# Four superblocks of 128-row tiles in place of two of 256-row tiles, with a shared PSUM bank and rows loaded eight tiles ahead

## The chip, the cores and the metric
The kernel runs on one core of a Trainium2 chip, in one launch. The metric is the device time in microseconds. All arithmetic is in 32-bit floats. The engines are TensorE (PE; its weight loads are PEld), VectorE (DVE), ScalarE (ACT), GpSimd (POOL) and SyncE (SP, which here only issues DMAs). TensorE writes to eight PSUM banks of 128 partitions by 512 floats.

## The reference
The input x is 32 batches of 128 rows by 128 features; the context is 32 x 120 x 128.
```python
x = x + tanh(g_xattn[0]) * attention(layernorm(x), ctx, ctx, ..., mask)   # 16 heads of 8, softmax over 120 keys
z = layernorm(x)                                        # 4096 rows
scores = z @ gate_w + gate_b                            # 8 experts
vals, idx = top_k(scores, 2); p = softmax(vals)
h = relu(einsum('td,edf->etf', z, w1) + b1)             # 512 hidden features
y = einsum('etf,efd->etd', h, w2) + b2
x = x + tanh(g_ffn[0]) * sum over the two experts of p * y
```
Only the two chosen experts of a row count, so 8192 pairs of row and expert have to be computed.

## The kernel before
**Attention.** The batches go in 8 groups of four (G). The work of a group is cut into 8 slots, t = 8G + s; a slot computes the scores of two units (a unit is four heads of one batch) and carries the two units of the slot before on. Scores go to one of four banks A, VectorE takes row maxima (`row_max`), ScalarE the exponentials (`exps`), TensorE transposes them (`transposes`, line 503) into bank T or U, and VectorE and ScalarE copy them to SBUF in turns (`copy_pt`). In odd slots TensorE multiplies a finished batch by the values (`values`, line 516) and sums (`sums`, line 524) into bank O; VectorE unloads O with a reciprocal (line 923) and a multiply (line 927, `unload`). Other small products of a group, such as projections, transposes of the next group and gate scores, are "entries" of given slots (`EXTRAS`).

**Routing.** Once group G is through attention, VectorE adds the residual and statistics, GpSimd normalises (`z2`), the gate scores pick two experts, and `route` gives each row a place in a DRAM buffer ordered by expert (`zs`). GpSimd scatters the 2 x 512 rows of a group with 8 indirect DMAs (line 809). Groups are joined into superblocks; before, two of four groups each (`SB = (4, 4)`). When the last group of a superblock is ranked, VectorE computes a table (`table`, lines 1008 to 1033) that says for each tile which expert and which rows it has. The number of tiles is fixed for the worst case: 23 tiles of 256 rows per superblock.

**Expert tiles.** SyncE waits for the table, then for each tile reads the expert and row from SBUF into registers, loads the expert's packed weights (`wbuf`, 578 KB, line 409) and the tile's rows (`zin`, 128 KB, line 413), four tiles ahead, and stores results to `ys` (line 420). TensorE transposes the rows into bank Y (line 577), VectorE moves them to `zT` (line 1040), TensorE multiplies by w1 (`first_product`, line 593) in two halves of two 128-feature chunks into bank U, ScalarE evicts with bias and relu into `H` (line 722), TensorE multiplies by w2 into Y (`second_product`, line 604), VectorE adds the bias (`yo`, line 1046). A tile is cut into four sub-steps, `sub(b, k)`.

**Order.** Every engine executes the same hand-written list of slots in its own program order; semaphores join them. The sub-steps of the first superblock are put into slots 42 to 71, three per slot. Attention's last scores are in slot 63; the slots up to 71 let the last group's routing drain. After slot 71 the rest of the first superblock and all 23 tiles of the second follow alone. In the first superblock's time U belongs to the experts, and attention is left with T alone; afterwards T is a second bank for first products. When all stores of a superblock have landed, GpSimd gathers for each of its batches and choices the 128 result rows (line 818), and VectorE adds them, weighted, to x (`combine`, line 1064); SyncE writes each finished group out. All gathers come after the slots, those of the second superblock after its last tile.

## Time and profile before
| | |
|---|---|
| median of 3 runs | 677.74 us (669.64 to 679.08) |
| profiled execution, whole | 671.73 us |
| its span, first to last instruction | 669.7 us |
| mean granted TensorE clock (1 is 2.4 GHz) | 0.911 |
| TensorE busy, share of the span | 527.6 us, 79% |
| VectorE busy | 290.7 us, 43% |
| ScalarE busy | 269.9 us, 40% |
| GpSimd busy | 256.7 us, 38% |
| moved by DMA | 78.75 MB, mean 118 GB/s |

The shares are means over stages: start, slots without expert work, slots with it, expert tiles alone, and gathers. An idle stretch of an engine is listed with what ended it; "issue" means that the profile shows nothing for which the engine waited. A group's "busy" counts overlapping instructions once, so that it can be less than count times mean.

### The profile page before, as it was taken

How to read it: one execution, taken by the hardware profiler on the slowest of the kernel's cores; microseconds unless marked ns; L12 is line 12 of the kernel's file. 1: busy time of each engine (PE TensorE's matmuls, PEld its weight loads, DVE VectorE, ACT ScalarE, POOL GpSimd, SP SyncE). 2: the span in 40 equal slices, each digit the busy share in tenths (PEclk: the TensorE clock that was granted, in tenths of full speed). 3: DMA queues.
4: the chain of work that ended last, by engine and by line, in shares of the span. 5: the costliest groups of instructions: out<-in, count | busy, mean ns of one | idle time of the engine just before them, and what ended most of it. 6: DMA issues, size and time to landing. Idle time of an engine off the chain costs nothing.

```text
span 669.7 us, 12645 instructions
## 1 busy us (share of the span) xinstructions
PE 527.6 (79%) x4481; PEld 379.2 (57%) x4481; DVE 290.7 (43%) x899; ACT 269.9 (40%) x812; POOL 256.7 (38%) x281
## 2 busy tenths in 40 slices
PE   1699999999989997898989898988838768878000
PEld 1265656566555654566767676676736667667000
DVE  2236648448557566344544555353331222321122
ACT  1256555446446552454555454642302333333000
POOL 6623063284454654332217022302453333200574
PEclk9779989789989986898999999999977999989655
DMA  5999790000000003311313131324426676663122
GB/s 127 285 418 241 244 374 2 17 17 11 9 17 18 2 17 84 123 52 52 119 53 116 55 120 54 119 70 154 133 71 209 202 208 207 206 174 122 51 82 71
DMA packets 60971, 78.75 MB, mean 118 GB/s; under 512 B 8421, under 2 KB 46573, under 8 KB 60909
## 3 DMA queue, kind: packets, MB, share of 16 engines
q1 hardware_dynamic: 56813, 69.55, 34.1%
q0 software_dynamic: 4096, 8.40, 4.1%
q8 instruction: 36, 0.59, 0.4%
q14 instruction: 26, 0.21, 0.1%
HBM read 46.73 MB, written 35.93 MB: 123 GB/s over the span
## 4 chain that ended last, share of the span: by engine, by line
PE 35%; issue 34%; SPq 13%; DMA 9%; POOL 4%; ACT 3%; DVE 2%; POOLq 0%; ACTq 0%
PE Y L604 11%; DMA zin<-zs 8%; PE U L593 7%; POOL yg L818 4%; SPq L391 4%; PE A L491 4%; PE T L503 3%; PE O L524 2%; PE A L495 2%; ACT H L722 2%; SPq L389 2%; PE T L593 2%; PE Y L577 1%; PE O L516 1%; SPq L386 1%
## 5 line engine op out<-in xcount | busy, mean ns | idle before, releaser
L687 ACT ACTIVATE P<-A,nmax 128x120 f32<-128x120 f32 x512 | 135.6, 386 | 13.8 <-DVE nmax L911 13.8
L911 DVE TENSOR_REDUCE nmax<-A 128x4 f32<-128x480 f32 x128 | 78.1, 652 | 110.2 <-PE A L495 96.2
L491 PE MATMUL A<-Kb,Q 32*128 32x480 f32 x256 | 102.3, 640 | 8.9 <-ACT P L687 6.1
L722 ACT ACTIVATE H<-U,wbuf 128x256 f32<-128x256 f32 x138 | 57.9, 471 | 121.0 <-PE U L593 118.3
L604 PE MATMUL Y<-wbuf,H 128*128 128x128 f32 x736 | 97.8, 285 | 9.4 <-issue 5.3
L809 POOL DMA_INDIRECT zs<-z,posu x64 | 63.2, 987 | 101.4 <-DVE posu L985 85.8
L604 PEld LDWEIGHTS Y<-wbuf,H 128*128 128x128 f32 x736 | 93.0, 199 | 15.9 <-issue 8.4
L818 POOL DMA_INDIRECT yg<-ys,ypos x64 | 60.4, 944 | 107.2 <-DMA ys<-yo 50.7
L593 PE MATMUL U<-zT,wbuf 128*128 128x256 f32 x276 | 74.6, 394 | 12.4 <-ACT H L722 11.7
L771 POOL TENSOR_TENSOR rstd<-mv,eps 128x4 f32<-128x4 f32 x16 | 3.2, 197 | 174.5 <-DVE mv L895 174.5
L503 PE MATMUL T<-I,P 128*120 128x128 f32 x352 | 55.9, 283 | 10.4 <-DVE PT L917 6.9
L593 PEld LDWEIGHTS U<-zT,wbuf 128*128 128x128 f32 x276 | 48.0, 194 | 20.6 <-ACT H L722 14.8
L503 PEld LDWEIGHTS T<-I,P 128*120 128x120 f32 x352 | 43.4, 144 | 22.8 <-issue 19.4
L917 DVE COPY PT<-T 120x512 f32<-120x512 f32 x64 | 43.8, 684 | 28.1 <-PE T L503 27.4
L1046 DVE TENSOR_TENSOR yo<-Y,wbuf 128x256 f32<-128x256 f32 x46 | 19.4, 423 | 81.0 <-PE Y L604 80.4
L491 PEld LDWEIGHTS A<-Kb,Q 32*128 32x128 f32 x256 | 30.3, 190 | 42.7 <-ACT P L687 28.4
L788 POOL TENSOR_SCALAR Kb<-Kt,hm 128x480 f32<-128x480 f32 x32 | 46.9, 1477 | 18.6 <-ACT Kt L708 18.6
L694 ACT COPY PT<-U 120x512 f32<-120x512 f32 x40 | 23.4, 586 | 74.0 <-PE U L503 65.2
L778 POOL TENSOR_SCALAR z<-X,mv,rstd 128x128 f32<-128x128 f32 x64 | 50.2, 791 | 3.0 <-POOL rstd L773 2.7
L495 PE MATMUL A<-mb_r,I_r 128*128 128x480 f32 x128 | 48.7, 464 | 0.0
L495 PEld LDWEIGHTS A<-mb_r,I_r 128*128 128x128 f32 x128 | 20.3, 199 | 48.0 <-issue 48.0
L1040 DVE COPY zT<-Y 128x256 f32<-128x256 f32 x46 | 19.4, 422 | 55.8 <-PE Y L577 50.4
(127 smaller groups left out, 613.3 us busy)
## 6 DMA issues: line engine op xcount, KB each, us to landing
wbuf<-wpk SPq DMA_DIRECT2D x46, 578.0 KB
zs<-zero SPq DMA_DIRECT2D x2, 9216.0 KB, 31.1
zin<-zs SPq DMA_DIRECT2D x46, 128.0 KB
ys<-yo SPq DMA_DIRECT2D x46, 128.0 KB
wpk<-in_w SPq DMA_DIRECT2D x1, 2048.0 KB, 35.0
wpk<-in_w SPq DMA_DIRECT2D x8, 256.0 KB, 10.7
out<-X SPq DMA_DIRECT2D x8, 256.0 KB
ctx_sb<-in_ctx SPq DMA_DIRECT2D x1, 1440.0 KB, 16.8
```

Source lines behind the costliest of these rows:

```text
L491: mm(a[:, 0:HG * LK].rearrange("p (j k) -> p j k", j=HG), Q[r, G % 2, i * LQ:(i + 1) * LQ], Kb[r, G % 2, :, i * LK:(i + 1) * LK], start=Tr ...
L495: mm(bank("S", n)[:, 0:HG * LK].rearrange("p (j k) -> p j k", j=HG), I_r[:], mb_r[:].unsqueeze(1).broadcast_to((128, HG, LK)), start=False ...
L503: last = nc.tensor.transpose(t[0:LK, j * LQ:(j + 1) * LQ], P[:, n % 4, j, :], I[:])
L593: last = mm(u_bank(b, half)[:, (c % 2) * TS:(c % 2 + 1) * TS], wbuf[:, n % NW, c * 128:(c + 1) * 128], zT[:, n % 2, :], start=True, stop=True)
L604: last = mm(Yb[:, h * 128:(h + 1) * 128], H[:, n % 2, c, h * 128:(h + 1) * 128], wbuf[:, n % NW, FF + c * D:FF + (c + 1) * D], start=(c == ...
L687: ins = nc.scalar.activation(P[:, n % 4, j, :], a[:, j * LK:(j + 1) * LK], ACT.Exp, bias=nmax[:, n % 4, j:j + 1])
L722: nc.scalar.activation(H[:, n % 2, c, :], u[:, (c % 2) * TS:(c % 2 + 1) * TS], ACT.Relu, bias=wbuf[:, n % NW, W_B1 + c:W_B1 + c + 1]).then ...
L778: ins = nc.gpsimd.tensor_scalar(dst[:, i, :], batch_x(G, i), mv[:, i, 0:1], r[:, 1, i:i + 1], ALU.subtract, ALU.mult)
L788: ins = nc.gpsimd.tensor_scalar(Kb[:, G % 2, j, :], Kt[:], hm[:, j:j + 1], None, ALU.mult)
L809: nc.gpsimd.indirect_dma_start(out=zs[sb_of(F)], out_offset=bass.IndirectOffsetOnAxis(ap=posu[:, F, k, i:i + 1], axis=0), in_=z2[:, F % 2, ...
L818: nc.gpsimd.indirect_dma_start(out=yg[:, n % NYG, :], out_offset=None, in_=ys[b], in_offset=bass.IndirectOffsetOnAxis(ap=ypos[:, i // GB, ...
L911: v.tensor_reduce(nmax[:, n % 4, :], bank("S", n)[:, 0:HG * LK].rearrange("p (j k) -> p j k", j=HG), AX_X, ALU.max, negate=True).then_inc( ...
```

## The change
There are four superblocks of two groups, and tiles have 128 rows. That gives 23 tiles per superblock and 92 in all. `SUBS`, `RATE` and `DRAIN_RATE` plan the steps: a tile has two, `first_product` (four chunks of 128 columns, one bank) and `y_step` (the second product of the tile before and the transpose of the rows two tiles on). Four steps go into an even slot, two into an odd one, and other numbers into slots 65 to 71. The first superblock starts in slot 26, the second in 42, the third in 58; 10 steps of the third and all of the fourth come after the slots.

`y_step` writes the upper half of bank O, whose lower half holds a batch's values and sums; so bank Y is gone and T has two banks, which attention alternates to the end. In the last steps, T's banks alternate with O and U. Before a step on O, TensorE waits for the unload of the last batch; before the values of a batch it waits until VectorE has emptied the last step. Weights are loaded five tiles ahead, rows eight, in separate functions; the next superblock's may be asked for during the last tiles of one. The two `zs` buffers are used in turns and are half as long. Of the gathers, 21 go into slots from 43 on, one per slot. In the last group of a superblock, rank, place and scatter come one slot earlier.
```diff
-SB = (4, 4)
+SB = (2, 2, 2, 2)
-TS = 256
+TS = 128
-NW = 4
+NW = 5
+NZ = 8
-SUBS = [4 * (n + 1) for n in NTB]
-SUB_FIRST = NS * (SB[0] + 1) + 2
-SUB_RATE = 3
+SUBS = [2 * (n + 1) for n in NTB]
+RATE = (4, 2)
+DRAIN_RATE = {65: 2, 66: 4, 67: 4, 68: 2, 69: 2, 70: 2, 71: 0}
...
-        Tb = ps("T")
+        Tb = [ps(f"T{r}") for r in range(2)]
         Ob = ps("O")
         Ub = ps("U")
-        Yb = ps("Y")
...
+        def u_bank(n):
+            return Tb[1] if late_tile(n) else Ub
+        def y_bank(m):
+            return Tb[0] if late_step(m) else Ob
...
             def transposes(n):
                 freed(pe, "S", n)
-                copied(pe, n - 2 if n <= LAST_U + 1 else n - 1)
+                copied(pe, n - 2)
...
                 pe.wait_ge(o_free, k + 1)
+                if begun["step"] is not None:
+                    wait(pe, yo_done, YO_THROUGH[begun["step"]])
+                    wait(pe, zt_done, ZT_THROUGH[begun["step"]])
...
+            def first_product(b, i):
+                n = N0[b] + i
+                pe.wait_ge(w_in[n % NW], 16 * (n // NW + 1))
+                pe.wait_ge(zt_done, zt_of(b, i))
+                ...
+                for c in range(NC):
+                    last = mm(u_bank(n)[:, c * TS:(c + 1) * TS], wbuf[:, n % NW, c * 128:(c + 1) * 128],
                               zT[:, n % 2, :], start=True, stop=True)
...
+            def y_step(b, i):
+                m, n = STEP[b, i], N0[b]
+                y = y_bank(m)
+                ...
+                if not late_step(m):
+                    pe.wait_ge(o_free, begun["batches"] + 1)
+                    begun["step"] = m
+                if moves_y(b, i):
+                    n = N0[b] + i - 1
+                    pe.wait_ge(h_done, NC * (n + 1))
+                    for c in range(NC):
+                        last = mm(y[:, 2 * TS:3 * TS], H[:, n % 2, c, :],
+                                  wbuf[:, n % NW, FF + c * D:FF + (c + 1) * D], start=(c == 0), stop=(c == NC - 1))
+                ...
+                elif moves_z(b, i):
+                    last = tile_transpose(y, N0[b] + i + 2, 3 * TS)
+                last.then_inc(y_ready, 1)
...
+            def load_w(n):
+                ...
+                wait(sp, yo_done, n - NW + 1)
+                e = sp.value_load(tab[0:1, b, 1, i:i + 1], min_val=0, max_val=NE - 1)
+                sp.dma_start(wbuf[:, n % NW, :], wpk[bass.ds(e, 1)].squeeze(0)).then_inc(w_in[n % NW], 16)
+            def load_z(n):
+                b, i = tile_of(n)
+                if i == 0:
+                    for q in range(2):
+                        sp.wait_ge(scat[q], 16 * 2 * GB * ((LAST[b] + 1 - q) // 2))
+                if n >= NZ:
+                    sp.wait_ge(zt_done, zt_of(*tile_of(n - NZ)))
+                row = sp.value_load(tab[0:1, b, 0, i:i + 1], min_val=0, max_val=ROWS - TS)
+                sp.dma_start(zin[:, n % NZ, :], zs[b % NZS][bass.ds(row, TS)]).then_inc(z_in[n % NZ], 16)
...
             for b in range(NB):
+                for i in range(-1, NTB[b]):
+                    if i >= 0:
+                        store(b, i)
+                    known = N0[b + 1]
+                    if b + 1 < NB and SLOT_OF.get((b, 2 * i + 3), NEVER) > NS * LAST[b + 1] + NS - 1:
+                        known = N0[b + 2]
+                    if i >= 0 or b == 0:
+                        while w_next < min(N0[b] + i + 1 + NW, known):
+                            load_w(w_next)
+                            w_next += 1
+                        while z_next < min(N0[b] + i + 1 + NZ, known):
+                            load_z(z_next)
+                            z_next += 1
...
# VectorE, in slot(G, s): moved behind routing and tables
+                for key in ks[1 if odd else 3:]:
+                    sub(*key)
+                if t in PRE:
+                    y_step(PRE[t], None)
+                for n in GATHER_AT.get(t - GATHER_LAG, ()):
+                    combine(n)
```

## Rows read from the trace of the kernel before

**Rows 1.** The timeline of VectorE: start, duration, engine, line, count, [idle before <-releaser].
```profile
170.49 0.95 DVE L923 RECIPROCAL orec<-O 128x128 f32<-128x128 f32 x1
226.81 0.96 DVE L923 RECIPROCAL orec<-O 128x128 f32<-128x128 f32 x1 [0.48 <-PE O L524]
...
266.63 0.96 DVE L923 RECIPROCAL orec<-O 128x128 f32<-128x128 f32 x1 [0.70 <-PE O L524]
...
457.87 0.96 DVE L923 RECIPROCAL orec<-O 128x128 f32<-128x128 f32 x1 [3.18 <-PE O L524]
```
**Rows 2.** Windows: stretch, length, each engine's busy time, granted clock, DMA share, GB/s.
```profile
170.50:227.00 56.50, 52.68 (x515) 32.75 (x514) 34.49 (x106) 30.41 (x98) 28.44 (x32) 0.97 0.03 11
335.70:446.70 111.00, 102.32 (x971) 76.31 (x972) 52.87 (x155) 56.72 (x174) 28.96 (x30) 1.00 0.28 86
505.50:621.30 115.80, 93.47 (x596) 80.94 (x596) 27.40 (x77) 38.45 (x92) 26.39 (x28) 0.97 0.61 185
```
**Rows 3.** The timeline of TensorE, one expert tile after the slots.
```profile
565.87 0.44 PE L577 MATMUL Y<-I,zin 128*128 128x128 f32 x2 [0.29 <-DMA zin<-zs]
566.14 1.03 PE L593 MATMUL T<-zT,wbuf 128*128 128x256 f32 x4
567.00 1.95 PE L604 MATMUL Y<-wbuf,H 128*128 128x128 f32 x16
568.79 1.03 PE L593 MATMUL U<-zT,wbuf 128*128 128x256 f32 x4
```
**Rows 4.** Waits by pair, 504 to 622 us: total, times, longest.
```profile
PE Y L577 <- DMA zin<-zs: 28.1, 16, 7.2
```
**Rows 5.** The timeline at the last tile's eviction and the next two gathers.
```profile
620.84 0.42 DVE L1046 TENSOR_TENSOR yo<-Y,wbuf 128x256 f32<-128x256 f32 x1 [2.21 <-PE Y L604]
623.92 0.94 POOL L818 DMA_INDIRECT yg<-ys,ypos  x1 [46.09 <-DMA ys<-yo]
625.17 0.94 POOL L818 DMA_INDIRECT yg<-ys,ypos  x1 [0.30 <-issue]
```
**Rows 6.** Waits of TensorE, 325 to 455 us.
```profile
PE U L593 <- ACT H L722: 6.5, 7, 1.2
PE Y L604 <- ACT H L722: 2.2, 4, 0.6
```
**Rows 7.** Costliest groups: line, shapes, count | busy, mean ns | idle before, releaser.
```profile
L687 ACT ACTIVATE P<-A,nmax 128x120 f32<-128x120 f32 x512 | 135.6, 386 | 13.8 <-DVE nmax L911 13.8
...
L503 PE MATMUL T<-I,P 128*120 128x128 f32 x352 | 55.9, 283 | 10.4 <-DVE PT L917 6.9
```
**Rows 8.** Groups by shape: the unload of bank O on VectorE.
```profile
L923 DVE RECIPROCAL orec<-O 128x128 f32<-128x128 f32 x32 | 30.6, 957 | 23.0 <-PE O L524 23.0
L927 DVE TENSOR_TENSOR OT<-O,orec 128x128 f32<-128x128 f32 x32 | 9.3, 292 | 1.1
```
**Rows 9.** The timeline around the first table.
```profile
252.13 0.21 DVE L1008 TENSOR_TENSOR tcmp<-jt,A 128x64 f32<-128x64 f32 x1
257.89 1.08 PE L503 MATMUL T<-I,P 128*120 128x128 f32 x4 [3.49 <-issue]
```
**Rows 10.** The timeline between the two superblocks.
```profile
485.12 0.17 DVE L985 CAST posu<-posf 128x8 uint32<-128x8 f32 x1
504.32 0.69 PE L577 MATMUL Y<-I,zin 128*128 128x128 f32 x2 [7.17 <-DMA zin<-zs]
```
**Rows 11.** The timeline of SyncE in the lone tiles: a store and the loads behind it.
```profile
599.72 0.37 SPq L420 DMA_DIRECT2D ys<-yo  x1
601.41 0.35 SPq L409 DMA_DIRECT2D wbuf<-wpk  x1
601.94 0.37 SPq L413 DMA_DIRECT2D zin<-zs  x1
```
**Rows 12.** SyncE's weight loads at the start of the second superblock.
```profile
502.02 0.35 SPq L409 DMA_DIRECT2D wbuf<-wpk  x1
504.59 0.02 SPq L409 DMA_DIRECT2D wbuf<-wpk  x1
507.51 0.00 SPq L409 DMA_DIRECT2D wbuf<-wpk  x1
```

More of the change, by code:

```diff
@@ L40 @@
 LAST = [SB0[b] + SB[b] for b in range(NB)]
-TS = 256
-TH = TS // 128
+TS = 128
 NTB = [(2 * n * TOK + NE * (TS - 1)) // TS for n in SB]
-N0 = [sum(NTB[:b]) for b in range(NB)]
+N0 = [sum(NTB[:b]) for b in range(NB + 1)]
 NTM = max(NTB)
 CAP = max(SB) * TOK
+NJ = CAP // TS
 ROWS = NE * CAP + NE * TS
+NZS = 2
 W_B1 = FF + NC * D
@@ L60, with slot_plan @@
 ZROW = 8 * D
-SUBS = [4 * (n + 1) for n in NTB]
-SUB_FIRST = NS * (SB[0] + 1) + 2
-SUB_RATE = 3
-LAST_U = 2 * (SUB_FIRST - 2) - 1
 DRAIN = NS * NG + NS
+NIT = 48
+SUBS = [2 * (n + 1) for n in NTB]
+RATE = (4, 2)
+DRAIN_RATE = {65: 2, 66: 4, 67: 4, 68: 2, 69: 2, 70: 2, 71: 0}
+NEVER = 10 ** 6
+def slot_plan():
+    subs, pre, t = {}, {}, 0
+    for b in range(NB):
+        k, t = 0, max(t, NS * (LAST[b] + 1) + 2)
+        if t < DRAIN:
+            pre[t - 1] = b
+        while k < SUBS[b] and t < DRAIN:
+            n = DRAIN_RATE.get(t, RATE[t % 2])
+            subs[t] = [(b, j) for j in range(k, min(k + n, SUBS[b]))]
+            k, t = k + n, t + 1
+    return subs, pre
@@ new lines, with moves_z, moves_y @@
+PLAN, PRE = slot_plan()
+SLOT_OF = {key: t for t, keys in PLAN.items() for key in keys}
+PLANNED = [sum(1 for key in SLOT_OF if key[0] == b) for b in range(NB)]
+STEPS = [(b, i) for b in range(NB) for i in [None] + list(range(NTB[b] + 1))]
+STEP = {key: m for m, key in enumerate(STEPS)}
+LATE = NS * NG + 2
+def moves_z(b, i):
+    return i is None or i + 2 < NTB[b]
+def moves_y(b, i):
+    return i is not None and i >= 1
+ZT_THROUGH = [sum(1 for key in STEPS[:m + 1] if moves_z(*key)) for m in range(len(STEPS))]
@@ new lines, with step_slot, late_step @@
+YO_THROUGH = [sum(1 for key in STEPS[:m + 1] if moves_y(*key)) for m in range(len(STEPS))]
+def step_slot(b, i):
+    if i is None:
+        return {c: t for t, c in PRE.items()}.get(b, NEVER)
+    return SLOT_OF.get((b, 2 * i + 1), NEVER)
+LATE_STEP = min(m for m, key in enumerate(STEPS) if step_slot(*key) >= LATE)
+LATE_TILE = min(N0[b] + i for b in range(NB) for i in range(NTB[b]) if SLOT_OF.get((b, 2 * i), NEVER) >= LATE)
+def late_step(m):
+    return m >= LATE_STEP and (m - LATE_STEP) % 2 == 0
@@ new lines, in late_tile, with prior, tile_of, zt_of @@
+def late_tile(n):
+    return n >= LATE_TILE and (n - LATE_TILE) % 2 == 0
+def prior(n, late):
+    return max([m for m in (n - 1, n - 2) if m >= 0 and late(m) == late(n)], default=None)
+def tile_of(n):
+    b = max(b for b in range(NB) if N0[b] <= n)
+    return b, n - N0[b]
+def zt_of(b, i):
+    return ZT_THROUGH[STEP[b, None if i < 2 else i - 2]]
+NGATHER = 2 * B
+GATHER_LAG = 3
+def gather_plan():
+    plan, n = {}, 0
+    for b in range(NB - 1):
+        ends = [SLOT_OF.get((b, k), NEVER) for k in range(SUBS[b])]
+        t = max(ends) + 2
+        while n < 2 * GB * LAST[b] and t + GATHER_LAG < NS * NG + 3:
+            c = min(GATHER_RATE, 2 * GB * LAST[b] - n)
+            plan[t] = list(range(n, n + c))
+            n, t = n + c, t + 1
+    return plan, n
@@ L589, in first_product @@
+                before = prior(n, late_tile)
+                if before is not None:
+                    pe.wait_ge(h_done, NC * (before + 1))
+                if n == LATE_TILE:
                     copied(pe, NG * NP - 1)
-                else:
-                    wait(pe, h_done, NC * n - 2 + 2 * half)
-                for c in (2 * half, 2 * half + 1):
-                    last = mm(u_bank(b, half)[:, (c % 2) * TS:(c % 2 + 1) * TS], wbuf[:, n % NW, c * 128:(c + 1) * 128],
+                for c in range(NC):
+                    last = mm(u_bank(n)[:, c * TS:(c + 1) * TS], wbuf[:, n % NW, c * 128:(c + 1) * 128],
@@ L800, in scatter @@
                 if part == 0:
-                    if F in SB0:
-                        pool.wait_ge(zs_clear[sb_of(F)], 16)
+                    b = sb_of(F)
+                    if F in SB0 and b < NZS:
+                        pool.wait_ge(zs_clear[b], 16)
+                    elif F in SB0:
+                        for q in range(NZ):
+                            pool.wait_ge(z_in[q], 16 * sum(1 for n in range(N0[b - NZS + 1]) if n % NZ == q))
                     pool.wait_ge(z2_done, F + 1)
@@ L836, in slot @@
                     residual_base(G)
[L837 removed]
+                for n in GATHER_AT.get(t, ()):
+                    gather(n)
+                if s == 6:
                     if G + 2 < NG:
```

306 lines of the change are left out of this document (134 added, 172 removed).

## The prediction
> **What bounds the kernel now.** I read the reciprocals of the attention batches first, because one falls in every second slot and so times the slots. Batches 11 and 16 stand 56.3 us apart, 11.3 us per pair of slots without expert work; batches 19 and 31 stand 191.2 us apart, 15.9 us per pair with six expert steps in it [rows 1]. Next the windows by stage. TensorE is busy 102.3 of 111.0 us in the filled slots and 52.7 of 56.5 us in the empty ones; VectorE, ScalarE and GpSimd are at half or less in the filled ones. After the slots TensorE falls to 93.5 of 115.8 us [rows 2]. So the slots are paced by TensorE's in-order queue, and an expert tile hidden in them is not free. A pair pays 15.9 - 11.3 = 4.6 us for 1.5 tiles of 256 rows, about 3.1 us a tile. In the second superblock's lone stage a tile takes 115.8 / 23 = 5.0 us, although its own TensorE work is shorter: transposes 0.27, two half first products of 0.86, second product 1.79, together 3.8 us [rows 3]. The rest is the wait for rows, 28.1 us in 16 waits [rows 4]. Last, the end: from the last eviction of an expert tile (ending 621.3) to the end of the span are 48.4 us, in which 32 gathers go out 1.25 us apart [rows 5].
>
> The profiled execution took 671.7 us, 669.7 of span and 2.0 around it. The median of the runs, 677.7, is 6.0 above it, and their own spread is 9.4; I sum against 671.7.
>
> **The change, part by part.**
>
> *Same rows, other places.* Both versions process 46 x 256 = 92 x 128 rows. With four superblocks the slots take expert work from slot 26 instead of 42, still three steps' worth of rows per two half tiles, and only 5 tiles of the third superblock and 23 of the fourth (28 x 128 rows) are left for the end, against 1.5 + 23 tiles of 256 before.
>
> *TensorE columns.* A first product now streams 128 columns per weight load instead of 256. Rows at 128 columns exist: 16 in 1.79 us is 0.112 us each; the 256-column ones take 0.86 / 4 = 0.215 [rows 3]. A 128-row tile therefore costs 0.14 + 8 x 0.112 + 8 x 0.112 = 1.93 us, two of them 3.86 against 3.78: +0.12 us per pair of slots.
>
> *First-product bank.* Four chunks of 128 fit one bank, so the second half no longer waits for the eviction of the first. That wait and the second product's like it cost 6.5 + 2.2 us in the 130 us from 325 to 455 [rows 6], 8.2 pairs: -1.06 us per pair.
>
> *Transpose banks.* The alternation of two banks stays where before one was left. In the filled slots of before the single one cost nothing visible (the wait on VectorE's copy is 6.9 us, in all such rows of the whole span [rows 7], and none of the idle time from 325 to 455), since expert work stands between. I take 0, bounds 0 and -7 us.
>
> *The shared bank.* This is the new wait. In an odd slot the expert step after the sums needs the unload: 0.47 us until VectorE starts [rows 1], 0.96 reciprocal, 0.29 multiply [rows 8], some 0.13 between and after: 1.85 us, less the entries placed ahead (estimated at 0.65 on average: four transposes, a projection or a gate product in three of four odd slots, one of some 0.3 in the last): 1.2 us. At the next odd slot the batch's values wait until VectorE has moved both halves of the last step: two operations of 128 columns (0.29 each, as that multiply) and two hand-overs, 1.0 us, less the transposes before it, 0.6: 0.4. Together +1.6 per pair. Behind the waiting TensorE instruction stands the next slot's transposes, hence both copies, hence scores; nothing overtakes. Bounds: 0 if the 2 us of slack in a pair swallow it, and 3.8 if VectorE reaches its moves only after statistics and routing in the same slot, 2 to 2.5 us later.
>
> A filled pair becomes 15.9 + 0.1 - 1.1 + 1.6 = 16.6 us (bounds 15.0 and 18.8). From batch 11 to batch 31 are 20 pairs, all filled: 332 us against 287.4 (170.5 to 457.9 [rows 1]), **+44.6**.
>
> *Tables.* A superblock's table runs on VectorE in one piece; TensorE waited 3.49 us while it ran from 252.1 [rows 9]. Two more of them fall in the slots (23 and 55; the one at 39 stood there already): **+7**. The fourth is where the second was.
>
> *Off the path.* ScalarE evicts 368 pieces of 128 columns; at the 135.6 / 512 = 0.265 us of the nearest shape [rows 7] that is +20 us on an engine half idle. The 21 gathers moved into slots take 26 us on GpSimd, which is busy 29 of 111 us there [rows 2]. Clearing half as much DRAM is hidden: nobody reads it before the slots begin to scatter. Weight traffic doubles to 0.89 MB per pair: 54 GB/s more, where the core moved 86 and moves 185 at the end [rows 2]. If these covers failed, GpSimd's 1.25 us per gather would show in its rows' due times.
>
> *After the slots.* From the last rank position (485.12) to the first rows landed and transposed were 19.2 us [rows 10]: eight scatters and a load. I keep them. Five tiles of the third superblock now cover part, but SyncE, in order, asks for the fourth's rows before it stores tile 19 and blocks until the scatters land; two output buffers let two or three tiles pass. So 26 tiles remain. Their pace: TensorE 1.93; SyncE's cycle of store, value loads and two loads, 599.72 to 602.31, is 2.6 us and does not shrink with the tile [rows 11]; the DMA took 2.57 and 2.92 us between weight loads when 706 KB per tile went back to back with gathers beside them [rows 12], and 578 + 64 + 64 = 706 KB is just what a small tile moves. SyncE thus paces 21 tiles (54.6 us), the last 5, already loaded, run at 1.93 (9.7), results cost 1, and half the tiles meet gathers at 0.3 more (4): 69.3. From rank position to last eviction: 19.2 + 69.3 = 88.5 against 136.2 (485.1 to 621.3), **-47.7**. Rows eight tiles ahead remove the 28.1 us of waits; late next is SyncE.
>
> *The last gathers.* 16 instead of 32 at 1.25 us [rows 5]: **-20**.
>
> Sum: 671.7 + 44.6 + 7 - 47.7 - 20 = 655.6, so **656 us**.
>
> **The rivals.**
> *The shared bank costs more (slower).* Place: the expert step after the sums and the values of the next odd slot. At 3.8 us of wait per pair the pair is 18.8: 656 + 20 x 2.2 = 700. It turns slower than the median of before from 1.1 us per pair beyond my 1.6. For it: the chain is serial and every slot's VectorE list holds other work. Against it: the empty slots already lose time to copies and maxima without TensorE idling long, and VectorE is half idle. If such waits also lowered the granted clock it would be dearer: it is 1.00 in the filled stage, 0.97 in the empty one [rows 2]. The Trainium skill (TensorE: Matmul & The Clock Gate, "A second HAM failure mode: psum-queue depth-cycling") says frequent short idles between bank turns can make the clock oscillate; nothing in the filled stage of before shows it. Chance 0.12.
> *The tail is paced by weights.* The weights of a tile are asked for five ahead but only after a store, about three tiles before use; if SyncE and a crowded queue make a tile 3.2 us, 26 x 0.6 = 15 more: 671. For it: 2.92 between loads in the burst. Against: TensorE, SyncE and DMA would have to queue instead of overlapping. Here the eight-ahead loads would not do what they say, being queued behind weights. Chance 0.17.
> *Halving the columns does not halve the product (slower).* If a 128-column product took what a 256-column one takes, 0.215 instead of 0.112, the first products would cost 92 x 8 x 0.103 = 76 us more: 732. Against it stand the second products, which are of just that shape and run at 0.112 [rows 3]. Chance 0.01.
> The Trainium skill (TensorE: Matmul & The Clock Gate, "Back-to-back issue gap") states a milder form: weight load and product together set the pace, about 81 ns at 128 columns and 131 at 512, so that columns in short products are dearer; by a line between the two points (an estimate, 98 ns at 256) the first products would grow by some 65%, about 50 us, and the kernel would end near 706. The rows at hand disagree.
> *The waits vanish in the slack.* A pair at 15.0 to 15.4, and the clock that stood at 0.97 where slots were empty goes to 1.00: 656 - 20 x 1.4 = 628. For it: work that fills a slot costs 4.6 us though it holds 5.7. Chance 0.2.
>
> **How the numbers follow.** The forecast gets 0.5, the others what stands beside them. The forecast's own range is 642 to 670. To hold eight in ten I reach to 628 at the low end and 686 at the high one. About 2% is what a measurement of this kernel can tell from no change: below 664 is faster, above 691 slower. Faster: 0.2 of the fast rival, 0.4 of the forecast, 0.02 of the tail rival, 0.62. Slower: 0.09 from the bank rival and 0.01 from the columns, 0.10. Within: 0.28.
>
> **What would show it.** In the profile after: reciprocals 16.6 us apart per batch from slot 26 on; waits of TensorE on the multiply of the unload, near 1.2 us, in odd slots, and short ones on the bias add or the copy; no wait of 1 us on the first product's eviction; granted clock at 1.00; a pause near 3.5 us at each of three tables; 26 or so tiles 2.6 to 2.9 us apart at the end with SyncE never idle for long; 28 us after the last eviction. Wrong if a pair takes over 17.7 us, if a tile at the end takes over 3.2, or if the last expert tile starts on time but its gathers find earlier ones still unsent.

## The result: 2.7% slower

The changed kernel takes 692.39 us (median of 4 runs, 686.63 to 698.28) against 678.41 for the kernel before (669.64 to 682.08): ratio 1.0267, interval [1.0188, 1.0347], which lies above 1 but not wholly above 1.02. Ratios, here and in the table below, come from the runs in the faster of the two states that the executions of a kernel fall into, so they are not quotients of the medians. The prediction was 656 with 686 as its upper end, so it was wrong in sign and outside its range. The profiled execution took 687.1 us, 685.3 of it span; the sum in the prediction was made against such an execution, and missed it by 31.5.

The page of the kernel after: engines, and the groups that answer to [rows 7].
```profile
span 685.3 us, 14478 instructions
PE 526.0 (77%) x4851; PEld 400.3 (58%) x4851; DVE 303.3 (44%) x1023; ACT 298.9 (44%) x996; POOL 258.7 (38%) x283
L840 ACT ACTIVATE H<-U,wbuf 128x128 f32<-128x128 f32 x300 | 85.8, 369 | 156.0 <-PE U L697 129.6
L723 PE MATMUL O<-wbuf,H 128*128 128x128 f32 x592 | 84.3, 288 | 46.6 <-DVE OT L1052 31.6
```
TensorE is busy as long as before (527.6), so its work did not grow; the span did. The reciprocals of batches 11 and 31, as in [rows 1]:
```profile
183.81 0.96 DVE L1048 RECIPROCAL orec<-O 128x128 f32<-128x128 f32 x1 [0.48 <-PE O L642]
...
539.66 0.96 DVE L1048 RECIPROCAL orec<-O 128x128 f32<-128x128 f32 x1 [3.25 <-PE O L642]
```
Against [rows 1, 5, 10] the span divides so (us):

| stretch | before | after | difference | predicted |
|---|---|---|---|---|
| start to batch 11 | 170.5 | 183.8 | +13.3 | +3.5, the table of slot 23 |
| batch 11 to 31 | 287.4 | 355.9 | +68.5 | +48.1 with the other table |
| batch 31 to last rank position | 27.2 | 21.9 | -5.3 | 0 |
| rank position to last eviction | 136.2 | 95.8 | -40.4 | -47.7 |
| last eviction to end | 48.4 | 27.9 | -20.5 | -20 |

The last two stretches came nearer to what was worked out. The loss lies in the slots, and there not in the ordinary pairs: from batch 12 to 17 they take 16.5, 17.1, 15.6, 17.0 and 16.5 us, where 16.6 was forecast. Five pairs take over 20 us. One is the pair from batch 11, 22.3 us, in which the first superblock starts; it comes up again below. The other four are 21.6 us from batch 9, 23.1 from 17, 20.7 from 22 and 28.6 from 25. Here is the one from batch 17, in the kernel after; first the windows, where the columns are those of [rows 2].
```profile
295.00:302.80 7.80, 7.45 (x81) 6.12 (x81) 3.73 (x12) 3.71 (x13) 4.15 (x6) 1.00 0.66 196
302.80:311.80 9.00, 4.04 (x37) 1.73 (x34) 1.22 (x2) 2.81 (x11) 5.66 (x6) 0.71 0.16 52
448.00:461.00 13.00, 2.37 (x14) 0.85 (x14) 1.22 (x2) 3.85 (x14) 8.32 (x9) 0.58 0.16 47
574.90:584.50 9.60, 0.00 (x0) 0.00 (x0) 0.04 (x1) 0.02 (x1) 6.67 (x8) 0.57 0.24 64
```
In 302.8 to 311.8 TensorE is busy 4.0 of 9.0 us and in 448 to 461 2.4 of 13.0, and VectorE and ScalarE are down with it; in the last row, from the expert tiles after the slots, all three stand still. Only GpSimd goes on. The timeline of the first of these pauses:
```profile
298.76 1.10 POOL L932 DMA_INDIRECT zs<-z,posu  x1 [2.74 <-DVE posu L1110]
...
300.03 1.16 PE L697 MATMUL U<-zT,wbuf 128*128 128x128 f32 x8
300.16 0.96 POOL L932 DMA_INDIRECT zs<-z,posu  x1 [0.30 <-issue]
...
302.69 0.96 POOL L932 DMA_INDIRECT zs<-z,posu  x1 [0.31 <-issue]
303.19 0.76 PE L642 MATMUL O<-PT,oneV 120*32 120x128 f32 x15
304.38 0.45 PE L642 MATMUL O<-PT,oneV 120*32 120x128 f32 x5 [0.43 <-issue]
305.83 0.46 PE L642 MATMUL O<-PT,oneV 120*32 120x128 f32 x5 [1.01 <-issue]
305.86 1.15 ACT L840 ACTIVATE H<-U,wbuf 128x128 f32<-128x128 f32 x4 [5.77 <-remote]
...
307.28 0.64 PE L642 MATMUL O<-PT,oneV 120*32 120x128 f32 x3 [0.99 <-issue]
307.30 1.22 DVE L1036 TENSOR_REDUCE nmax<-A 128x4 f32<-128x480 f32 x2 [7.91 <-remote]
...
308.70 1.09 PE L642 MATMUL O<-PT,oneV 120*32 120x128 f32 x3 [0.78 <-issue]
309.02 0.96 POOL L932 DMA_INDIRECT zs<-z,posu  x1 [0.30 <-issue]
```
Nine indirect DMAs go out 1.27 us apart from 298.76 to 309.02. From the fifth on, TensorE issues the 32 products of one batch's sums in portions of 15, 5, 5, 3, 3 and 1, some 1.45 us apart, waiting for nothing that the profile shows. ScalarE evicts at 305.86 a product that ended at 301.2: the word of it came 4.6 us late. The pause ends some 2 us after the last of the DMAs. The clock suffers too: it is 0.71 in the window of the pause, and 0.84 in the whole pair behind it. The pauses named here all lie in such runs: nine DMAs from 158.7, nine from 298.8, seven from 380.4 (gathers and scatters in turn), thirteen from 442.4, seventeen from 562.6. The kernel before has runs of at most four in its slots, except the one of eight at its table, from 253.0 to 262.0.

### The profile page after: what moved, and what is told of

Same layout as the page of the kernel before. It is cut to its first block, busy times and chain, and to the rows that moved or that the text cites. A ratio compares the mean times of both kernels' runs of the same rounds, so it can differ in the third digit from the quotient of the medians.

```text
span 685.3 us, 14478 instructions
## 1 busy us (share of the span) xinstructions
PE 526.0 (77%) x4851; PEld 400.3 (58%) x4851; DVE 303.3 (44%) x1023; ACT 298.9 (44%) x996; POOL 258.7 (38%) x283
## 4 chain that ended last, share of the span: by engine, by line
PE 56%; DVE 9%; issue 9%; SPq 9%; DMA 6%; another core or an unknown queue 5%; POOL 4%; ACT 2%; POOLq 0%; ACTq 0%; DVEq 0%
PE A L606 10%; PE U L697 9%; PE O L723 8%; PE T L617 7%; PE A L610 5%; PE O L642 5%; PE O L634 4%; DVE orec L1048 3%; ACT P L804 2%; SPq L509 2%; DMA ys<-yo 2%; SPq L521 2%; PE O L704 2%; SPq L520 2%
## 5 line engine op out<-in xcount | busy, mean ns | idle before, releaser
L840 ACT ACTIVATE H<-U,wbuf 128x128 f32<-128x128 f32 x300 | 85.8, 369 | 156.0 <-PE U L697 129.6
L804 ACT ACTIVATE P<-A,nmax 128x120 f32<-128x120 f32 x512 | 136.3, 390 | 11.3 <-DVE nmax L1036 11.2
L723 PE MATMUL O<-wbuf,H 128*128 128x128 f32 x592 | 84.3, 288 | 46.6 <-DVE OT L1052 31.6
L723 PEld LDWEIGHTS O<-wbuf,H 128*128 128x128 f32 x592 | 75.8, 200 | 54.7 <-issue 54.0
L606 PE MATMUL A<-Kb,Q 32*128 32x480 f32 x256 | 87.7, 657 | 13.6 <-DVE tcmp L1133 7.4
L697 PE MATMUL U<-zT,wbuf 128*128 128x128 f32 x600 | 88.2, 293 | 11.5 <-issue 6.0
L697 PEld LDWEIGHTS U<-zT,wbuf 128*128 128x128 f32 x600 | 78.5, 204 | 18.7 <-issue 10.7
L617 PE MATMUL T<-I,P 128*120 128x128 f32 x512 | 84.1, 291 | 2.5 <-DVE PT L1042 2.5
L811 ACT COPY PT<-T 120x512 f32<-120x512 f32 x64 | 37.6, 587 | 97.8 <-PE T L617 87.6
L617 PEld LDWEIGHTS T<-I,P 128*120 128x120 f32 x512 | 66.6, 147 | 14.9 <-issue 8.2
L1048 DVE RECIPROCAL orec<-O 128x128 f32<-128x128 f32 x32 | 30.6, 958 | 45.9 <-PE O L642 25.9
L610 PEld LDWEIGHTS A<-mb_r,I_r 128*128 128x128 f32 x128 | 20.5, 201 | 49.4 <-issue 49.4
L642 PE MATMUL O<-PT,oneV 120*32 120x128 f32 x1024 | 42.4, 292 | 6.6 <-issue 6.5
L634 PE MATMUL O<-PT,Vm 120*32 120x128 f32 x1024 | 36.4, 285 | 13.9 <-DVE yo L1176 12.7
## 6 DMA issues: line engine op xcount, KB each, us to landing
wpk<-in_w SPq DMA_DIRECT2D x8, 256.0 KB, 11.6
```

What stands on the lines that cost most here:

```text
L606: mm(a[:, 0:HG * LK].rearrange("p (j k) -> p j k", j=HG), Q[r, G % 2, i * LQ:(i + 1) * LQ], Kb[r, G % 2, :, i * LK:(i + 1) * LK], start=Tr ...
L610: mm(bank("S", n)[:, 0:HG * LK].rearrange("p (j k) -> p j k", j=HG), I_r[:], mb_r[:].unsqueeze(1).broadcast_to((128, HG, LK)), start=False ...
L617: last = nc.tensor.transpose(Tb[n % 2][0:LK, j * LQ:(j + 1) * LQ], P[:, n % 4, j, :], I[:])
L634: mm(Ob[32 * j:32 * j + 32, 0:LQ], Vm[:, G % 2, i * HG + j, 32 * g:32 * g + 32], PT[:, (NHG * k + g) % NPT, j * LQ:(j + 1) * LQ], start=(g ...
L642: last = mm(Ob[32 * j:32 * j + 32, LQ:2 * LQ], oneV[:, g, :], PT[:, (NHG * k + g) % NPT, j * LQ:(j + 1) * LQ], start=(g == 0), stop=(g == ...
L697: last = mm(u_bank(n)[:, c * TS:(c + 1) * TS], wbuf[:, n % NW, c * 128:(c + 1) * 128], zT[:, n % 2, :], start=True, stop=True)
```

## The experiments

The kernels ran on four chips, here called 2, 3, 13 and 4; kernels on one chip share the runs of the kernel before, and medians are compared within a chip. The changed kernel itself did not run on chip 2.

| chip | kernel | median us | before there | ratio, interval |
|---|---|---|---|---|
| 2 | scatters spaced | 662.89 | 666.73 | 0.9887 [0.9851, 0.9923] |
| 2 | spaced, gathers too | 661.91 | 666.73 | 0.989 [0.9838, 0.9941] |
| 2 | gathers after the slots | 650.87 | 666.73 | 0.9729 [0.9675, 0.9782] |
| 2 | before, runs of eight | 665.32 | 666.73 | 0.9976 [0.9943, 1.0009] |
| 3 | changed kernel | 694.75 | 671.77 | 1.0337 [1.0274, 1.0401] |
| 3 | gathers late, rows asked first | 692.51 | 671.77 | 1.0257 [1.0174, 1.0339] |
| 3 | own bank for the second product | 676.09 | 671.77 | 1.0044 [1.001, 1.0077] |
| 3 | before, rows eight ahead | 647.65 | 671.77 | **0.9619 [0.9515, 0.9723]** |
| 13 | changed kernel | 691.3 | 676.85 | 1.0218 [1.0136, 1.03] |
| 13 | scatters spaced | 680.27 | 676.85 | 1.0064 [1.0019, 1.0109] |
| 13 | gathers late, pause behind eight | 685.22 | 676.85 | 1.0113 [1.0023, 1.0203] |
| 13 | before, runs of eight | 720.27 | 676.85 | **1.0679 [1.0585, 1.0774]** |
| 4 | own bank, scatters spaced | 659.93 | 674.61 | 0.9826 [0.9777, 0.9875] |
| 4 | before, rows eight ahead, spaced | 655.81 | 674.61 | 0.9735 [0.9653, 0.9816] |
| 4 | slots' DMAs spaced | 672.68 | 674.61 | 0.998 [0.9939, 1.0022] |

**First: spacing, and late gathers.** The theory was that long runs of indirect DMAs make the pauses; the rival, that the tables and the shared bank do. In the first kernel a GpSimd operation of about 1 us stands behind each scatter of a superblock's last group, so that scatters go out 2.3 us apart. The second does the same behind each gather of the first three superblocks. The third leaves all gathers until after the slots.
```diff
+                        if parts == 1:
+                            nc.gpsimd.tensor_tensor(fill[:, next(fills), :], eps4[:], mhalf4[:], ALU.pow)
```
```diff
+                if n < 2 * GB * SB0[NB - 1]:
+                    nc.gpsimd.tensor_tensor(fill[:, next(fills), :], eps4[:], mhalf4[:], ALU.pow)
```
```diff
-GATHER_AT, GATHERED = gather_plan()
+GATHER_AT, GATHERED = {}, 0
```


> The changed kernel, with one operation of about 1.0 us put on GpSimd behind each of the eight scatters that go out in one run at a superblock's end, so that they follow 2.3 instead of 1.27 us apart. Theory 1 (a long run of indirect DMAs on GpSimd holds up TensorE's signals: the stalls of 6 to 9 us at 165, 303, 448 us and part of that at 575): the three stalls in the slots go or shrink to under 2 us each, 15 to 20 us are won against 692, less up to 8 for the scatters that land later: 675 to 683. Theory 2 (the superblock's table and the shared bank make the pauses, the scatters only stand beside them): pauses stay, the scatters land 8 us later each, 692 to 702.

> As e1_paced, and the same operation also behind each gather but the last superblock's 16, so that no run of indirect DMAs follows closer than 2.2 us before the last gathers. Theory 1: also the pause of 9.5 us at 575 and the 2.8 at 388 go, 5 to 10 us below e1_paced: 668 to 678. Theory 2: as e1_paced or slower, 692 to 705.

> The changed kernel with none of the 21 gathers in the slots; all 64 come after the slots, 18 more of them uncovered at the end or so. Theory 1: the pause at 388 (scatters and gathers in turns) goes and that at 442 to 461 loses its second half, -8 us, but at the end some 18 more combines follow the last tile at 1.25 us: +20; about 702. Theory 2: nothing won in the slots, 712. If the end is not lengthened, theory 1 gives 684.

All three came out faster than before and below what was expected of them, which looked like a clear win for the theory, but it was not. The kernel with late gathers still has runs of nine scatters, and its trace on chip 2 shows no pause in them: the pairs from batches 9, 17 and 25 take 14.2, 15.6 and 15.5 us, and from rank position to last eviction are 88.3 us, as predicted. Chip 2 shows no pauses for spacing to remove, and spacing the gathers too adds nothing. There spacing costs: the pairs in which a superblock starts, from batches 11, 19 and 27, take 27.0, 24.7 and 22.2 us with scatters spaced and 20.1, 17.4 and 18.8 in the kernel with late gathers, since the rows land later.

**The same runs put into the kernel before.** The scatters of every group go out as one run of eight in slot 7, nothing else changed.
```diff
-                if G >= 2 and G - 1 not in LAST:
-                    scatter(G - 2, s, NS)
...
-                    if G >= 1 and G in LAST:
+                    if G >= 1:
```


> The kernel before with every group's eight scatters sent in one run in slot 7 (before, only the last group of a superblock has that; the six others send one per slot). Theory 1: six more runs of eight, each a pause of 4 to 8 us: 678 plus 24 to 48, 702 to 726. Theory 2: no change beyond 1%, 672 to 685.

> The kernel before with all groups' scatters in runs of eight. Theory 1 on a chip where c3_after pauses: each of the runs inside the slots costs 4 to 8 us, +20 to +45 on before. If the pause needs more than a run, such as expert steps' own signals or other loads beside it, at most the three runs in filled slots cost, +0 to +20.

On chip 2 it made no difference; on chip 13 the same kernel lost 43 us. The windows of one run, first half and what follows, on chip 13:
```profile
173.00:177.80 4.80, 4.80 (x63) 3.13 (x62) 2.29 (x7) 3.08 (x10) 3.89 (x4) 1.00 0.15 44
177.80:187.00 9.20, 5.01 (x30) 2.69 (x27) 2.56 (x4) 1.43 (x4) 3.90 (x5) 0.65 0.11 36
```
and of the same instructions on chip 2:
```profile
166.70:171.50 4.80, 4.80 (x74) 3.37 (x76) 3.45 (x9) 3.58 (x11) 3.89 (x4) 1.00 0.14 44
171.50:180.70 9.20, 8.66 (x83) 5.14 (x74) 5.62 (x18) 5.87 (x20) 5.11 (x7) 1.00 0.12 37
```
Both run alike for four DMAs. Then the first issues 30 products where the second issues 83, and its clock falls to 0.65. TensorE on chip 13 in that stretch:
```profile
177.19 0.63 PE L524 MATMUL O<-PT,oneV 120*32 120x128 f32 x13
178.77 0.45 PE L524 MATMUL O<-PT,oneV 120*32 120x128 f32 x5 [0.94 <-issue]
180.23 0.43 PE L524 MATMUL O<-PT,oneV 120*32 120x128 f32 x5 [1.01 <-issue]
181.68 1.10 PE L524 MATMUL O<-PT,oneV 120*32 120x128 f32 x4 [1.02 <-issue]
```
These are the portions of the changed kernel, in a kernel with neither shared bank nor tables in those slots. Of the seven pairs with a run, six are 6.7 to 7.4 us longer than on chip 2 (14.9 against 8.2 from batch 6, 22.3 against 15.5 from batch 22), some 42 us in all. So the runs make the pauses, on some chips; DMA traffic as such does not, as it moves 36 GB/s there and 37 here.

The seventh is an exception. The run at the table, eight scatters from 281.1 to 290.1, leaves its pair at 16.4 us on chip 13 against 16.5 on chip 2, and TensorE shows no portions in it, by its windows and the timeline:
```profile
281.00:285.80 4.80, 1.54 (x11) 1.19 (x10) 4.37 (x16) 1.07 (x2) 3.74 (x4) 1.00 0.13 41
285.80:292.50 6.70, 6.40 (x46) 3.63 (x46) 2.70 (x8) 2.12 (x8) 4.06 (x5) 0.55 0.48 139
286.03 0.68 PE L503 MATMUL T<-I,P 128*120 128x128 f32 x4 [3.48 <-issue]
```
TensorE stands still for 3.48 us there, but so it does on chip 2, where the trace names VectorE's copy behind the table as the releaser. What differs from the paused runs is that TensorE issued only 11 products during the first four DMAs, and 63 in the run from 173. No run tests whether that is the reason; a run of eight does not always make a pause, even on a chip that has them.

**Spacing on a chip with pauses.** The changed kernel, the spaced one, and one with late gathers on chip 13. In the last, four operations were meant to part the eight scatters into fours; as written they stand only behind all eight, so it tells of late gathers with runs kept, not of fours.
```diff
+                if parts == 1 and i % 2:
+                    for _ in range(4):
+                        nc.gpsimd.tensor_tensor(fill[:, next(fills), :], eps4[:], mhalf4[:], ALU.pow)
```


> The changed kernel, as the measure for the runs beside it on their chip. If long runs of indirect DMAs hold up TensorE only on some chips, the pairs of slots with the runs of nine and of thirteen take 21 to 29 us here or 14 to 16, and the ratio is about 1.03 or about 0.98 with them.

> The changed kernel with the eight scatters of a superblock's end 2.3 us apart. Theory 1 (a run that follows 1.27 us apart holds up TensorE's signals from its fifth on): where c3_after has pairs of 21 to 29 us at such a run, this has 14 to 16, and it is 15 to 25 us faster than c3_after; its start pairs of a superblock are some 5 us longer, because the scatters land later. Theory 5 (the pauses are a property of the chip at any pace): the same pauses, no gain.

> The changed kernel with no gathers in the slots and a pause of 5 us on GpSimd behind each four scatters of a superblock's end, so that no run in the slots is longer than four or five. Theory 1: no pair over 17 us at the scatters on any chip, 25 to 35 us under c3_after where that has the pauses; within 8 us of the late-gathers kernel where not. Theory 5: the pauses stay.

Windows of the same pair, from batch 17 to 18, in the changed kernel:
```profile
288.40:311.60 23.20, 17.18 (x154) 12.26 (x154) 10.77 (x51) 8.55 (x32) 13.19 (x15) 0.92 0.29 87
```
and with scatters spaced:
```profile
283.80:300.20 16.40, 14.76 (x154) 11.76 (x154) 10.89 (x52) 9.26 (x35) 10.11 (x12) 1.00 0.32 94
```
The same 154 products take 16.4 instead of 23.2 us. The pairs from 9, 17 and 25 fall from 21.9, 23.2 and 28.8 us to 15.2, 16.3 and 16.1, 26.3 us together, and the median falls by 11 (the two profiled executions differ by 18.9), less than the 15 to 25 expected. Part of the gain is lost again because the scatters land later: the pairs from 10, 19 and 26 grow by 4.1, 3.2 and 4.5 us. After the slots the spacing neither costs nor gains much there: 98.4 us from the last rank position to the last eviction against 96.9 with the pause. On chip 2, without a pause, it costs 9.9 (98.2 against 88.3), and TensorE waits 15.5 us before the last superblock's first rows; the releaser named had long been done.
```profile
PE T L706 <- DVE yo L1180: 15.5, 1, 15.5
```
The late gathers with runs of eight keep pairs of 18.9, 22.1 and 22.1 us; they are rid only of the run of seven at batch 22 (23.6 to 15.9) and of part of the thirteen.

**The changed kernel again, and which loads SyncE asks for first.** The second edit takes the gathers out of the slots and lets rows go ahead of weights.
```diff
+                    sp.wait_ge(table_step, NTAB * b + TAB_AT)
...
-                        while w_next < min(N0[b] + i + 1 + NW, known):
-                            load_w(w_next)
-                            w_next += 1
                         while z_next < min(N0[b] + i + 1 + NZ, known):
                             load_z(z_next)
                             z_next += 1
+                        while w_next < min(N0[b] + i + 1 + NW, known):
+                            load_w(w_next)
+                            w_next += 1
```


> The changed kernel itself, beside the kernel before on the chip of these runs. Theory 3 (the pauses of 6 to 9 us at 165, 303, 388, 448 and 575 us belong to the changed kernel's own mix of gathers and scatters on GpSimd): they stand here too and it is slower than before by 1 to 3%. Theory 4 (the pauses came with the conditions of the one execution or chip, not with the kernel's order): no pause longer than 3 us in the slots, and a ratio of 0.96 to 0.98 with reciprocals 16.0 us apart, as in e2_late_gathers.

> The changed kernel with no gather in the slots (as e2_late_gathers) and SyncE asking for rows ahead of weights, where both are due. If the first rows of a superblock wait behind five weight loads (the pair with the first superblock's start took 20 to 27 us), 5 to 8 us are won on e2_late_gathers: ratio 0.960 to 0.967. If that wait is for the scatters alone, nothing: 0.970 to 0.976.

The pauses are in both traces: pairs of 21.7, 23.1 and 28.6 us in the changed kernel, and of 21.8, 23.3 and 23.0 without gathers in the slots. The same late gathers on chip 2 had 14.2, 15.6 and 15.5. So the runs of scatters alone are enough, and the gathers account for the longer pause from batch 25 and the one from 22 (15.8 us here). Asking for rows first gained nothing that shows: the pair from batch 11 takes 24.4 us, and TensorE waits 5.4 us for weights in it.

**The shared bank.** The second product and the row transposes get a bank of their own again, and attention is left with one transpose bank.
```diff
-        Tb = [ps(f"T{r}") for r in range(2)]
+        Tb = [ps("T")] * 2
...
+        Yb = ps("Y")
...
-                if begun["step"] is not None:
-                    wait(pe, yo_done, YO_THROUGH[begun["step"]])
-                    wait(pe, zt_done, ZT_THROUGH[begun["step"]])
```


> The changed kernel with the second product and the transposed rows in a bank of their own and attention on one transpose bank throughout, as before the change. If the shared bank costs the 1.6 us per pair that the prediction took and one transpose bank costs nothing where expert work fills the slots, 20 pairs give 32 us less than a_after; if what the bank saves is lost again in waits for the one transpose bank, within 5 us of it.

It is 18.7 us faster than the changed kernel on the same chip, between the two outcomes that were expected. The pauses stay (22.2, 24.1, 30.4 us); ordinary pairs fall from about 16.1 to 14.9. TensorE's waits from 325 to 455 us in the kernel after,
```profile
PE O L634 <- DVE yo L1176: 7.3, 6, 3.6
PE O L723 <- DVE OT L1052: 5.7, 7, 1.3
```
are gone in it, and what the single transpose bank costs there is small:
```profile
PE T L618 <- DVE PT L1037: 1.5, 2, 1.3
```
Ahead of the expert steps it is not small. From the start to batch 11 this kernel takes 198.0 us against 186.8 for the changed one, and the pair from batch 5, for example, 15.0 against 9.6. From batch 11 to 31 it takes 334.2 against 357.3. So 23.1 us are gained in the filled slots and 11.2 lost before them; these two executions differ by 13.3 us in span.

**Rows eight ahead, alone.** In the kernel before, `zin` gets eight buffers and its own load function; tiles, superblocks, banks and weights (four ahead) stay.
```diff
+NZ = 8
-        zin = sb("zin", [128, NW, TH, D])
+        zin = sb("zin", [128, NZ, TH, D])
...
-                    load(b, i)
+                    if i < NW:
+                        load_w(b, i)
+                    load_z(b, i)
...
-                        load(b, i + NW)
+                        load_w(b, i + NW)
+                    if i + NZ < NTB[b]:
+                        load_z(b, i + NZ)
```


> The kernel before with the rows of a tile loaded eight tiles ahead, weights four as before: only this part of the change. If the 28 us of waits for rows in the lone tiles go, and weights or SyncE come next at 4.2 us a tile of 256 rows, 15 to 20 us less: ratio 0.970 to 0.978. If the weights are as late as the rows, nothing: 0.995 to 1.005.

This has the lowest ratio to before of all kernels here: 3.8% faster, more than the 2.2 to 3.0% expected. The 28.1 us of waits [rows 4] are down to one, before the first tile, and the window that answers to the third of [rows 2] has TensorE busy 90.0 of 92.1 us:
```profile
PE Y L585 <- DMA zin<-zs: 7.1, 1, 7.1
501.00:593.10 92.10, 90.03 (x598) 80.95 (x598) 27.80 (x78) 38.51 (x92) 27.43 (x29) 0.97 0.79 236
```
A lone tile takes 92.1 / 23 = 4.0 us instead of 5.0, near the 3.8 of TensorE's own work.

**Do the two causes add?** Own bank and spaced scatters (not the last superblock's) together; the changed kernel with all DMAs in slots spaced; and the kernel before with rows eight ahead and its one run of eight spaced.
```diff
+                        if parts == 1 and F < NG - 1:
+                            nc.gpsimd.tensor_tensor(fill[:, next(fills), :], eps4[:], mhalf4[:], ALU.pow)
...
+                if n < GATHERED:
+                    nc.gpsimd.tensor_tensor(fill[:, next(fills), :], eps4[:], mhalf4[:], ALU.pow)
```
The second part of the edit is in the changed kernel's version alone.

> The changed kernel with the second product back in a bank of its own (one transpose bank) and, behind each of the 8 scatters of the first three superblocks' last groups, one GpSimd power of 128x4 of about 1 us. If the pauses come from long uninterrupted runs of indirect DMAs and the shared bank's cost is a separate term, both gains add: on a chip with pauses -19 us for the bank (as own bank against the changed kernel) and -12 to -15 us for the spacing, so a ratio to before of 0.975 to 0.985, with no pair of 21 us or more at batches 9, 17 and 25, and ordinary filled pairs near 15 us. If the shared bank's waits and the pauses are the same time counted twice, spacing on top of the own bank brings under 5 us: ratio 0.995 to 1.005. On a chip without pauses, 0.96 to 0.975.

> The changed kernel with the power of about 1 us behind each end-of-superblock scatter of the first three superblocks and behind each of the 21 gathers in slots, but not behind the last superblock's eight scatters. Theory 'long runs': all pauses in the slots go (pairs at batches 9, 17, 25 at 15 to 17 us) while the last rows land as early as in the changed kernel, so it is 6 to 9 us better than the version spaced everywhere was against before on a chip with pauses: ratio 0.99 to 1.00. If the last run of scatters pauses TensorE in the tail as much as its later landing cost, nothing is won over spacing everywhere: 1.005.

> The kernel before with rows loaded eight tiles ahead (weights four), and the scatters of its first superblock's last group spaced by a GpSimd power of about 1 us each. Gain of the rows alone: about 5 us fewer per... 1 us fewer per lone tile, 24 tiles, ratio 0.96. The kernel before has one run of eight scatters in its slots and no visible pause there, so theory 'long runs' says the spacing adds 0 to -5 us: ratio 0.955 to 0.965. If spacing itself cost time on GpSimd, the ratio would be 0.97 or more.

The two gains add in the first: 0.9826, within the 0.975 to 0.985 expected, with pairs of 17.3, 17.1 and 17.9 us from batches 9, 17 and 25. With only the slots spaced the ratio is 0.998, as expected, against 1.0064 on chip 13 with the last run spaced too; that is across chips. Between these two kernels of one chip are 12.8 us, but they differ in more than the bank: the first has its gathers unspaced, and its pair from batch 22, with a run of seven, takes 19.4 us against 15.6. The pause after the slots is still in both (TensorE and VectorE do nothing from 543.1 to 552.7 in the first). The third kernel missed: 0.9735 against the 0.955 to 0.965 expected. The pair from batch 19, in which its first superblock starts, takes 25.7 us, where the version not spaced has 19.5 on chip 3: where a superblock is waiting for its scatters, spacing them costs.

## Why the prediction was wrong

**The step that failed** is "Off the path": "The 21 gathers moved into slots take 26 us on GpSimd, which is busy 29 of 111 us there". GpSimd did have the time. What the step left out is what a long run of its indirect DMAs does to the others; the sum had no term for it. The change makes such runs: a superblock's last group scatters all eight at once three times in the slots instead of once, gathers come between them, and rank positions are early. The four pairs with a pause cost about 21.6 - 14.2, 23.1 - 15.6, 20.7 - 15.6 and 28.6 - 15.5 over the kernel with late gathers on chip 2: 33 us, and the pause after the slots 7.5 more (95.8 against 88.3). This compares across chips, and it is more than the 31.5 missed, so other terms were too dear. That runs cause the pauses is shown twice: put into the kernel before they cost 43 us on chip 13; spaced in the changed kernel they let the same 154 products take 16.4 us instead of 23.2. Most of it comes from the scatters, which the prediction's step does not name: with no gather in the slots the pauses from batches 9, 17 and 25 remained on chips 3 and 13.

**A smaller miss** lies ahead of slot 26. Rank, place and scatter one slot earlier were costed at nothing, and the table that now stands in slot 23 at 3.5 us. But VectorE now routes and counts in the slot in which TensorE needs the counts, and then runs the table where no expert step covers it. In the kernel with late gathers on chip 2, which has no pauses:
```profile
156.30 0.25 PE L673 MATMUL A<-Mh,tri 128*128 128x32 f32 x1 [2.06 <-DVE CU L1099]
...
149.00:156.30 7.30, 5.24 (x55) 3.57 (x47) 5.05 (x36) 3.05 (x10) 2.71 (x4) 0.89 0.01 2
156.30:164.90 8.60, 8.34 (x82) 5.26 (x83) 4.33 (x10) 3.42 (x13) 5.79 (x8) 0.60 0.07 24
...
171.48 1.08 PE L617 MATMUL T<-I,P 128*120 128x128 f32 x4 [2.47 <-DVE PT L1042]
171.50:176.50 5.00, 5.00 (x41) 2.76 (x42) 2.21 (x7) 2.12 (x8) 0.00 (x0) 0.50 0.92 311
```
TensorE stood still for 2.06 us and the granted clock over the next 8.6 is 0.60, so that much of it is at 1.2 GHz. Behind the table it stood still for 2.47 us more, and the clock is 0.50 behind it. Batch 11 comes at 180.2 there, 8.2 after the kernel before with runs on that chip (172.0): the pair from batch 9 takes 14.2 us against 9.6 and the one from 10, with the table, 15.2 against 8.2, while batch 9 had come 3.4 earlier. The Trainium skill (TensorE: Matmul & The Clock Gate, "A second HAM failure mode: psum-queue depth-cycling") speaks of frequent short idles between groups of products making the clock oscillate. These windows show a fall behind two single idles of 2.06 and 2.47 us; the filled slots from batch 12 to 27, with many shorter waits, stand at 0.99 in that trace, so there the rule cost nothing.

**The shared bank** was right in kind and near in size: +1.6 us per pair forecast, about 1.2 measured, by ordinary pairs of 16.1 against 14.9 us on chip 3 and by 23.1 us over the 20 pairs. The second transpose bank, kept where before one was left, was costed at 0; the kernel that has one bank from the start pays 11.2 us ahead of batch 11, a stretch in which the kernel before has two as well. Where it was expected, TensorE waits on the unload's multiply and on the bias add, and the rival of 3.8 us per pair did not happen.

**The filled pair** was too dear on the whole: 16.6 was forecast for each. The kernel with late gathers on chip 2 has 320.4 us from batch 11 to 31, tables included, against 335.5 forecast (332 and one table): 15.1 too many, which partly hid the misses above. The ordinary pairs from batch 12 to 17 and from 20 to 25 take 15.2 to 17.0 us; the last ones, from 28 on, take 15.6, 13.6 and 11.6, where the forecast took the mean of before for every pair. Products of 128 columns ran eight in 1.06 us at full clock, as [rows 3] said. The Trainium skill (TensorE: Matmul & The Clock Gate, "Back-to-back issue gap") would have made them dearer per column, the first products by about 65% as estimated in the prediction; the trace disagrees here. They are busy 107.7 us against 99.3, 8% more, at a mean clock of 0.896 against 0.911, and TensorE's whole busy time is 526.0 us against 527.6.

**Tables** cost nothing that shows where expert steps fill the slots: the pairs that hold them, from batches 18 and 26, take 14.5 and 14.2 us in that kernel, and the one from 22, at the same place in its group and without a table, 15.6. The pair from batch 10, in empty slots, paid for its table as above. (The sum has one table too few: its 332 us use the mean of the pairs behind slot 39, and so hold no table of that slot.) What the sum had no term for is the start of a superblock. The pairs from 11, 19 and 27, in which one starts, take 20.1, 17.4 and 18.8 us there, 1 to 4 above 16.6, and 22.3, 17.1 and 19.2 in the kernel after. In the first of them TensorE waits for rows, 1.9 us and 3.6, and its clock is 0.80 and 0.77.

**After the slots** the 88.5 us were right where no pause came (88.3 on chip 2) and 95.8 with one. SyncE paces the tiles as forecast: its cycle in the kernel after,
```profile
600.12 0.33 SPq L510 DMA_DIRECT2D wbuf<-wpk  x1
601.22 0.33 SPq L521 DMA_DIRECT2D zin<-zs  x1
601.60 0.43 SPq L527 DMA_DIRECT2D ys<-yo  x1
602.78 0.33 SPq L510 DMA_DIRECT2D wbuf<-wpk  x1
```
is 2.66 us for a tile of 128 rows, when no output store falls between. The last gathers came to 27.9 as forecast. What the sum did not ask is what rows eight ahead would do without the small tiles: 24 us of gain, more than the whole change was forecast to bring.

**Left open.** Why runs of indirect DMAs hold up TensorE's issue and its signals, and why not on chip 2. The profile names no releaser ("issue", "remote"). On each chip a kernel was profiled once, so that a cause that changes from one loading of a program to the next, rather than from chip to chip, is not excluded; on chips 3, 13 and 4 every kernel that had long runs beyond those at the table and the end of the kernel before paused, and none of the three with such runs on chip 2. Why the run of eight at a table made no pause is open as well. No kernel with fours in the scatters of a last group was run, so where between four and eight it begins is known only from runs that started to pause at their fifth.

## What to carry to other kernels

Look at the work that a change bunches, not only at how much of it there is: the scatters of the kernel before cost nothing visible in their places, and in runs of eight some 7 us a run on a chip that pauses. Spread GpSimd's indirect DMAs in groups of at most four, as the kernel before does, or with other work between, except where someone waits for the last of them. And try the parts of a change one by one: the deeper row loads alone gave 3.8%, and the rest of the change took away more than that.

## What the runs showed of the hardware

- Runs of seven to seventeen indirect DMAs of GpSimd, 1.27 us apart, held up TensorE on chips 3, 13 and 4 and on that of the first result, in the run read in full from the fifth DMA until about 2 us after the last. TensorE then issued three to five small products every 1.45 us, and ScalarE began 4.6 us after the end of the product that it evicted. On chip 2 the same instructions showed none of it, and the run of eight at the table of the kernel before showed next to none in the four traces that have it, chips 2, 3 and 13 and that of the first result.
- Chips differ: the kernel before took 666.7, 671.8, 674.6 and 676.9 us on the four of them, and the kernel with runs of eight 665.3 on one and 720.3 on another.
- A stop of 2.06 us in TensorE was followed by 8.6 us at a mean granted clock of 0.60, and one of 2.47 us by 5.0 us at 0.50.
